# Inverse deviations of the norm tails by a power on GpSimd in place of a root on ScalarE and a reciprocal on VectorE

## The reference, cut to what matters

```python
def _layernorm(x, axis=-1, eps=1e-05):
    m = jnp.mean(x, axis=axis, keepdims=True)
    v = jnp.var(x, axis=axis, keepdims=True)
    return (x - m) / jnp.sqrt(v + eps)

x = _layernorm(x + gradient_ffn(x))        # series terms + SwiGLU, width 1248
x = _layernorm(x + expert_loras(x))        # base matrix + softmax-weighted sum of 8 low-rank experts
x = _layernorm(x + values_attention(x))    # attention on a sequence of length 1: only values remain
x = _layernorm(x + quantised_swiglu(x))    # int weights, zeros and scales, 14 tiles of 128
x = _layernorm(x + conv_stack(x))          # 4 layers of norm, decaying rotation scan, small MLP
x = _layernorm(x + two_loras(x))
x = _layernorm(x + causal_attention(x))    # 32 heads, one key head
x = _layernorm(x + scaled_swiglu(x))       # int weights with one scale, 11 tiles of 128
```

## Time and profile before

| | us |
|---|---|
| runs | 1475.19, 1478.64, 1481.58 |
| median | 1478.64 |
| the profiled execution, its own time | 1483.27 |
| its span (first to last instruction) | 1481.6 |
| matmuls of TensorE (PE) busy | 1285.3 (87%) |
| weight loads of TensorE (PEld) busy | 843.9 (57%) |
| VectorE (DVE) busy | 754.6 (51%) |
| ScalarE (ACT) busy | 426.6 (29%) |
| GpSimd (POOL) busy | 142.2 (10%) |

### The profile page before, as it was taken

The page is one execution under the profiler, slowest core; times in us unless marked ns, Lnnn a source line. Parts: engine busy times, 40 slices in busy tenths (PEclk is TensorE's granted clock), DMA queues, the critical chain, the costliest instruction groups (busy, mean ns, idle before and its releaser), DMA issues. The chain is left out here.

```text
span 1481.6 us, 14589 instructions
## 1 busy us (share of the span) xinstructions
PE 1285.3 (87%) x5314; PEld 843.9 (57%) x5314; DVE 754.6 (51%) x1301; ACT 426.6 (29%) x709; POOL 142.2 (10%) x208
## 2 busy tenths in 40 slices
PE   7999997869799999973565698989999999699998
PEld 4787664324378887763443243444554553388877
DVE  5223323792655554423556563877777642433254
ACT  2122111100221214210221213136656666312141
POOL 0000000490000000001111004000101114000000
PEclk9999998889989999985566699989999999799999
DMA  7110002450066540004000001000000000021001
GB/s 304 43 42 0 0 0 71 196 195 0 5 222 220 208 153 0 1 15 141 1 0 0 0 0 43 1 1 2 1 2 2 3 3 1 24 83 64 21 19 38
DMA packets 18681, 78.82 MB, mean 53 GB/s; under 512 B 3330, under 2 KB 4226, under 8 KB 16452
## 3 DMA queue, kind: packets, MB, share of 16 engines
q1 hardware_dynamic: 18628, 78.13, 14.6%
HBM read 75.76 MB, written 2.10 MB: 53 GB/s over the span
## 5 line engine op out<-in xcount | busy, mean ns | idle before, releaser
L346 PE MATMUL psum<-L_ffn_x,L_ffn_w_up 128*128 128x512 f32 x1200 | 277.1, 394 | 16.2 <-DVE L_ffn_x L475 16.2
L346 PEld LDWEIGHTS psum<-L_ffn_x,L_ffn_w_up 128*128 128x128 f32 x1200 | 228.4, 191 | 64.5 <-issue 16.6
L1751 DVE TENSOR_REDUCE mqa_top<-psum 128x1 f32<-128x512 f32 (+3 forms) x304 | 186.0, 656 | 59.8 <-PE psum L1577 40.1
L1670 ACT ACTIVATE mqa_prob<-psum 128x512 f32<-128x512 f32 x288 | 160.1, 601 | 87.6 <-PE psum L1595 86.7
L363 PE MATMUL psum<-L_ffn_wd,L_ffn_part_h 128*128 128x512 f32 x600 | 141.6, 397 | 7.0 <-DVE L_ffn_wd L298 7.0
L1595 PE MATMUL psum<-mqa_stack,mqa_keys 100*128 100x512 f32 x288 | 132.7, 475 | 4.7 <-DMA mqa_stack<-mqa_rows 3.4
L363 PEld LDWEIGHTS psum<-L_ffn_wd,L_ffn_part_h 128*128 128x128 f32 x600 | 114.3, 192 | 31.6 <-DVE L_ffn_part_h L289 7.8
L1571 PE MATMUL psum<-mqa_keys,mqa_stack 96*128 96x512 f32 (+3 forms) x384 | 129.3, 384 | 2.3 <-DVE mqa_top L1751 1.0
L346 PE MATMUL psum<-L_attn_x,L_attn_w_up 128*128 128x512 f32 x480 | 111.3, 394 | 3.9 <-DVE L_attn_hidden L464 3.9
L346 PEld LDWEIGHTS psum<-L_attn_x,L_attn_w_up 128*128 128x128 f32 x480 | 91.2, 190 | 23.8 <-issue 4.8
L464 DVE TENSOR_TENSOR L_ffn_hidden<-L_ffn_gate,psum 128x512 f32 (+1 forms) x50 | 34.3, 686 | 138.3 <-PE psum L346 138.3
(11 more groups left out here) (237 smaller groups left out, 1611.0 us busy)
## 6 DMA issues: line engine op xcount, KB each, us to landing
L_ffn_stage<-in_L_w SPq DMA_DIRECT2D x25, 768.0 KB, 6.6
L_ffn_z_int<-in_L_z SPq DMA_DIRECT2D x14, 768.0 KB, 4.4
L_ffn_s_all<-in_L_s SPq DMA_DIRECT2D x14, 768.0 KB, 6.1
lora_wo<-in_L_wo SPq DMA_DIRECT2D x8, 1024.0 KB, 4.9
L_attn_stage<-in_L_w SPq DMA_DIRECT2D x10, 512.0 KB, 3.6
L_attn_w_down<-in_L_down SPq DMA_DIRECT2D x1, 2560.0 KB, 24.8
x_feat<-in_x_feat SPq DMA_DIRECT2D x2, 1024.0 KB, 7.1
x_tok<-in_x_tok SPq DMA_DIRECT2D x1, 2048.0 KB, 19.2
```

The lines of the kernel that those rows point to most:

```text
L346: ins = nc.tensor.matmul(bank[half][:, :], w_up[:, slot, w_part, at:at + P], x[:, x_part, k, half * HALF:(half + 1) * HALF], start=k == 0 ...
L1670: nc.scalar.activation(prob[:, n % PROBS, :], score_bank[n % 3], ACT.Exp, scale=SCALE)\
L1751: nc.vector.tensor_reduce(top[:, i % 2, lo // HALF, heads[0]:heads[-1] + 1], max_bank[n % 3][:, 0:len(heads) * width] .rearrange("p (h k) ...
```

## The change

Every tail except that of the experts takes its inverse deviation from GpSimd. There an addition computes var + eps, a wait follows for this addition, and a power of -0.5 gives `rstd`; VectorE waits for that and normalises at once, without a reciprocal. The blocks of the three SwiGLUs and of the two LoRAs get a GpSimd program for it; in `conv_stack` it is appended to GpSimd's program, and in the block of experts and values it stands after the rotation table. The expert tail, which runs while GpSimd builds the rotation table, keeps the root on ScalarE and the reciprocal on VectorE. The constant -0.5 moves from the causal attention to `setup`.

```diff
@@ class Tail
+    def __init__(self, chip, out_bank, tr_bank, last=False, root_on_act=False):
...
@@ def dve
-        dve.wait_ge(self.std_ready, self.base + t + 1)
-        step(nc.vector.reciprocal(c.rstd[:, t:t + 1], c.std[:, t:t + 1]))
+        dve.wait_ge(self.rstd_ready, self.base + t + 1)
+        if self.root_on_act:
+            step(nc.vector.reciprocal(c.rstd[:, t:t + 1], c.std[:, t:t + 1]))
         nc.vector.tensor_scalar(row, row, c.mean_var[:, t, 0:1], c.rstd[:, t:t + 1],
                                 ALU.subtract, ALU.mult).then_inc(self.normed, 1)
@@ def act_std
-                             bias=c.eps[:, 0:1]).then_inc(self.std_ready, 1)
+                             bias=c.eps[:, 0:1]).then_inc(self.rstd_ready, 1)
+
+    def pool(self, pool):
+        c, nc = self.c, self.c.nc
+        for t in range(NT):
+            pool.wait_ge(self.var_ready, self.base + t + 1)
+            nc.gpsimd.tensor_tensor(c.std[:, t:t + 1], c.mean_var[:, t, 1:2], c.eps[:, 0:1], ALU.add)\
+                .then_inc(self.var_eps, 1)
+            c.var_eps += 1
+            pool.wait_ge(self.var_eps, c.var_eps)
+            nc.gpsimd.tensor_tensor(c.rstd[:, t:t + 1], c.std[:, t:t + 1], c.half_power[:, :], ALU.pow)\
+                .then_inc(self.rstd_ready, 1)
@@ def act
         for t in range(NT):
-            self.act_std(act, t)
+            if self.root_on_act:
+                self.act_std(act, t)
@@ def setup
             nc.gpsimd.memset(c.eps[:, :], EPS)
+            nc.gpsimd.memset(c.half_power[:, :], -0.5)
@@ def swiglu
+            @block.gpsimd
+            def _(pool):
+                tail.pool(pool)
...
                     if t + 1 < NT:
                         split_h(act, t + 1, 1, 0)
-                    tail.act_std(act, t)
                     if t + 2 < NT:
                         split_h(act, t + 2, 0, 0)
@@ def lora_then_single_key
-        tail = Tail(c, c.bank[4:6], c.bank[6:8])
+        tail = Tail(c, c.bank[4:6], c.bank[6:8], root_on_act=True)
...
                 c.rot.pool(pool)
+                tail_values.pool(pool)
@@ def causal_attention
-        half_power = sb("half_power", [P, 1])
...
-                nc.gpsimd.memset(half_power[:, :], -0.5)
```

More of the change, by code:

```diff
@@ L51, in __init__ @@
         self.ffn_base["loaded"] = [0, 0]
-        self.tails = self.ln_count = 0
+        self.tails = self.ln_count = self.var_eps = 0
         psum = ctx.enter_context(nc.psum_tensor("psum", [P, 8, 512], F32))
@@ L63 @@
 class Tail:
-    NAMES = ("out_ready", "out_taken", "ln_step", "var_ready", "std_ready", "normed", "transposed", "feat_ready")
-    def __init__(self, chip, out_bank, tr_bank, last=False):
+    NAMES = ("out_ready", "out_taken", "ln_step", "var_ready", "var_eps", "rstd_ready", "normed", "transposed",
+             "feat_ready")
+    def __init__(self, chip, out_bank, tr_bank, last=False, root_on_act=False):
         self.c, self.out_bank, self.tr_bank, self.last = chip, out_bank, tr_bank, last
-        (self.out_ready, self.out_taken, self.ln_step, self.var_ready, self.std_ready, self.normed,
+        self.root_on_act = root_on_act
+        (self.out_ready, self.out_taken, self.ln_step, self.var_ready, self.var_eps, self.rstd_ready, self.normed,
          self.transposed, self.feat_ready) = chip.tail_sems
@@ L154, in setup @@
     nc = c.nc
-    c.eps = c.sb("eps", [P, 1], F32)
+    c.eps, c.half_power = c.sb("eps", [P, 1], F32), c.sb("half_power", [P, 1], F32)
     ready, zeroed = c.sem("const_ready"), c.sem("ident_zeroed")
@@ L1509, in _ @@
                         pool.wait_ge(pool_step, i + 1)
-                        nc.gpsimd.tensor_tensor(c.rstd[:, qt:qt + 1], c.std[:, qt:qt + 1], half_power[:, :], ALU.pow)\
+                        nc.gpsimd.tensor_tensor(c.rstd[:, qt:qt + 1], c.std[:, qt:qt + 1], c.half_power[:, :], ALU.pow)\
                             .then_inc(std_ready, 1)
```

## The result

The changed kernel took 1484.53 us, the median of 12 runs (1480.70 to 1490.68), beside 1478.01 for the kernel before in as many runs. The ratio is 1.0046 with a 95% interval of 1.0032 to 1.0059: 4.7 to 8.7 us slower, against +8.2 in the forecast. That is just inside the 0.5% which the prediction called no change; the interval, 0.32% to 0.59%, reaches across this bound.

A forecast was written before the change was run, and what follows sets the result against it. TensorE's matmuls were busy in 87% of the span, but the change was taken to touch a chain, not an engine's load. 0.38 + 0.38 + 3.04 + 2.77 + 1.2 + 0.38 = 8.15, taken as +8.2: 1486.8 us, range 1482.4 to 1491.2.

The forecast's parts named there:

- The price of the link: Start of variance to start of normalisation, in every changed tail: 1.12 us in place of 0.74, so 0.38 longer.
- Gradient, value and last SwiGLU tails: In each of these three tails only the last tile pays for the longer link: +0.38 us each.
- Quantised SwiGLU: Second SwiGLU's tail: all eight weight loads waited in a closed loop, so all eight links show, +3.04 us.
- Convolution tail: VectorE sets the pace and sits in each link: 3.04 less 0.27 waited for TensorE, +2.77 us.
- Two-LoRA tail: Stepping through the tiles gave 31.7 us in place of 30.5: +1.2, between bounds of 0.38 and 3.04.
- Table loads at nothing: ScalarE at tails and convolution loop: eight loads, 10.3 us, perhaps vanish; costed at nothing because ScalarE idled behind them.
- The rival that rested on them: ScalarE's loads, convolution loop and four tails, were on the path: up to 10.3 us back, 1476.5 us; chance 6%.
- The swallowed middle: Rival: inner links of second SwiGLU (2.66) and two-LoRA tail (0.8) are hidden; +4.7 us, 1483.3; chance 18%.
- The clock: Rival: convolution tail's longer gaps keep TensorE at 1.2 GHz into the two-LoRA stage; 2.5 us more, 1489.3; chance 13%.
- The chance: Whole kernel: 0.52 for slower by over 0.5%, 0.45 for within 0.5%, 0.03 for faster.
- The signs of being wrong: Second SwiGLU's waits stay at 0.47, link is not 1.12, or a stage without a tail changes by over 2 us.
- nothing to collide with: In the changed tails VectorE waits during the link, so GpSimd's two small operations meet no VectorE work.

The follow-up runs named there:

- late_turns: Changed kernel with TensorE's transposes of the previous tile moved behind the second half of each SwiGLU's product; 1482.26 us, ratio 1.0035.
- late_turns_root: Kernel before, root kept, with TensorE's transposes of the previous tile moved behind the second half of each SwiGLU's product; 1477.41 us, ratio 0.9984.
- idle_roots: Changed kernel with ScalarE's roots put back in every tail as dead work, bringing back eight table loads; 1485.11 us, ratio 1.0038.
- only_swiglu2: Kernel before with GpSimd's power in the quantised SwiGLU alone, root and reciprocal in all other tails; 1481.37 us, ratio 1.0029.
- ahead_root: Kernel before with later SwiGLU transposes; convolution tail adds and measures the next tile before normalising, products one tile further ahead; 1469.30 us, ratio 0.9938.
- ahead_gpsimd: Changed kernel with later SwiGLU transposes; convolution tail adds and measures the next tile before normalising, products one tile further ahead; 1474.22 us, ratio 0.9977.

## Why the prediction was right

**The price of the link** was exact: 1.12 us in the changed tails, 0.38 more, from four rows of a stage that did it already. Nothing else was priced, so the rest was only a question of where it shows.

**Gradient, value and last SwiGLU tails**, one link each: 0.4, 0.4, 0.4 against 0.38. The value tail's first tile had 0.43 of slack for 0.38, and its pace stayed at 3.87.

**Quantised SwiGLU**, 3.04 forecast, 3.1 by the trace, alone and in the whole. That the weight loads had waited 0.47 in every tile was the reading which carried this term; `late_turns` and `late_turns_root` show that it was the loop and not another engine.

**Convolution tail**, 2.77 forecast, 2.6 by the trace. The small rest is that the period grew by 0.37 and not 0.38, and that the one long period of before was 3.00, so 0.35 and not 0.27 above the others.

**Two-LoRA tail**, 1.2 forecast, 1.2 by the trace, between bounds of 0.38 and 3.04. Neither the busy share nor the period alone would have given it.

**Table loads at nothing**: eight of the nine loads of the earlier trace rows went, four at roots and four in the convolution's loop, as foreseen, and `idle_roots` shows that they had cost nothing. The rival that rested on them falls. The Trainium skill, page "ScalarE: Activation LUTs", section "What ACT_TABLE_LOAD costs", adds a drain of about 1.38 us to each. No run here shows one: in `idle_roots` the load at 817.92 starts 0.02 us after ScalarE's activation before it ended, and the earlier trace rows have an activation 0.01 behind a load.

**The swallowed middle** falls by `only_swiglu2` and the two-LoRA rows.

**The clock** was half right: it fell, and cost almost nothing. The windows of TensorE in the changed kernel, the first 16 products of the two LoRAs and the convolution tail (us, busy of PE, PEld, DVE, ACT, POOL, granted clock, DMA, GB/s), and behind them the products by the timeline:

```profile
851.00:861.00 10.00, 9.59 (x16) 3.78 (x16) 2.78 (x6) 0.00 (x0) 0.73 (x2) 0.75 0.00 0
816.00:841.00 25.00, 19.95 (x45) 8.93 (x44) 15.38 (x31) 4.58 (x8) 5.86 (x16) 0.50 0.00 0
...
850.88 9.71 PE L629 MATMUL psum<-two_w_eff,x_feat 128*128 128x512 f32 x16 [0.78 <-DVE two_w_eff L871]
```

In the convolution tail the clock now stays at 1.2 GHz throughout (0.77 in the same window before). Over this whole tail the granted clock is 0.50 in all four kernels that have the power in it and VectorE's old order, and 0.82, 0.73 and 0.66 in the three with the root and that order; so the longer gaps of TensorE go with it, though what lowers the clock is argued. It costs nothing there, since VectorE sets the pace. The two-LoRA stage starts nearly as before, 9.71 us for its first 16 products (the window cuts off the first 0.12) against 9.53: 0.2 us where I had priced 2.5.

**The chance** leaned the wrong way by a little: I gave 0.52 to slower by over 0.5% and 0.45 to within, for a forecast of 0.55%; measured is 0.46%. The sum was 8.2 and the tails give 8.1, so no term failed; the medians give 6.5.

**The signs of being wrong.** Two of the three did not show: the waits left 0.47, and the link is 1.12. The third did: stretches that the change leaves alone differ by more than 2 us between the two profiles. From the last normalisation of the quantised SwiGLU to the first addition of the convolution tail it was 163.3 us before and 159.9 after, and from the end of the two-LoRA tail to the first addition of the last SwiGLU 537.5 and 535.0. The sign was badly chosen, as these stretches vary by as much between kernels that are alike there; the next paragraph has the figures.

**What stays open** is what lies between tails and time. Stages that no kernel here touches differ from profile to profile: the layers of the convolution stack take 28.4 to 30.5 us each, from the end of the two-LoRA tail to the first addition of the last SwiGLU it is 535.0 to 538.1. The window of one layer shows it, 720 to 750 us with the same 72 matmuls, in the kernel before (columns as for the windows above):

```profile
720.00:750.00 30.00, 17.95 (x72) 12.66 (x72) 17.51 (x43) 6.77 (x9) 4.56 (x7) 0.61 0.00 0
```

and in the changed kernel:

```profile
720.00:750.00 30.00, 16.03 (x72) 11.98 (x72) 19.29 (x47) 5.49 (x8) 5.47 (x7) 0.67 0.00 0
```

With a granted clock of 0.67 in place of 0.61 the matmuls take 1.9 us less, and from the Silu of this layer to that of the next it was 28.4 us in place of 30.4. All ten profiles agree with this. The whole stretch ahead of the convolution tail, with the same 367 matmuls, takes 159.1 to 160.0 us at a granted clock of 0.61 in three of them (the changed kernel, `only_swiglu2`, `ahead_root`), with TensorE busy for 85.1 to 85.9; in the other seven it takes 163.0 to 164.7 at 0.58 to 0.59, busy for 88.7 to 89.9. Each group has kernels with the power and with the root in the tails, and with and without the loads in the loop. The runs of the changed kernel go the same way: six with a mean clock of 0.910 to 0.911 took 1480.7 to 1484.7 us, six with 0.906 to 0.907 took 1484.4 to 1490.7. So a kernel can gain or lose a few us outside the stages that its edit touches. That would cover `ahead_root` (9.2 faster by ratio, 7.5 by the medians, 5.4 by its tails), `ahead_gpsimd` (3.4 faster by ratio, 4.8 by its tails), `late_turns` (5.2 slower, 2.5 by its tails) and the 1.6 of the change itself, which the expert tail would cover as well. What sets the clock in these layers, and whether an edit elsewhere shifts it, is not shown: no run held the clock fixed.

## What to carry to other kernels

Before an operation moves to an idle engine, measure the link, from the start of what feeds it to the start of what needs it, semaphore hops and all; busy time says only part of it (0.29 + 0.16 became 0.19 + 0.55, 0.29 more, while the link grew from 0.74 to 1.12, 0.38 more). Then ask in each stage for the waits ahead of the consumer: no wait means one link per stage, a wait in every tile means one per tile, and slack smaller than the growth has to be stepped through. And where the link shows, reordering the work around it (the next tile's statistics ahead of this tile's normalisation, the transposes behind the second half) was worth about as much as the choice of engine, and made that choice matter less. In the quantised SwiGLU it took 2.1 us off the tail with the root and 5.0 with the power, and the 3.1 between the two engines became 0.3; in the convolution tail it took off 2.7 and 7.3, and the power, 2.6 behind before, was 2.0 ahead.

## What the runs showed of the hardware

GpSimd's addition on 128x1 took 0.40 us where VectorE's normalisation ran beside it, against 0.19 where VectorE waited (`ahead_gpsimd` and the changed kernel). Beside VectorE's addition, which takes one of its operands from PSUM, it took 0.19 too (first tile of that tail in `ahead_gpsimd`), and the power took 0.54 there as everywhere. The prediction's "nothing to collide with" held only because VectorE stood still. Two powers in a row without a wait between them start 0.50 us apart though each lasts 0.54. The same 72 matmuls of a convolution layer cost 1.9 us more or less with the granted clock, in an unchanged stage (17.95 at 0.61, 16.03 at 0.67).
